# Attention heads divided before their output projection, two heads projected together, and value projections in rounded passes

## The reference

```
xn  = layernorm(x)
out = x + attention(xn) + ffn(xn)
```

## Time and profile before

| | |
|---|---|
| median of 3 runs (lowest, highest) | 1462.79 us (1461.44, 1465.05) |
| profiled execution, own time | 1463.13 us |
| its span, first to last instruction | 1461.4 us |
| mean clock granted to TensorE | 0.958 |
| PE, DVE, ACT, POOL busy, share of the span | 92%, 71%, 65%, 59% |
| DMA: bytes moved, mean rate | 72.47 MB, 50 GB/s |

### The profile page before, as it was taken

One profiled execution on the slowest core, in us unless ns is written; L12 is line 12 of the kernel. 1 busy time (PEld: TensorE's weight loads), 2 busy tenths in 40 slices (PEclk: granted clock), 3 DMA queues, 4 the chain that ended last, 5 costly groups with the idle time before them and its releaser, 6 DMA issues.

```text
span 1461.4 us, 27770 instructions
## 1 busy us (share of the span) xinstructions
PE 1351.4 (92%) x8360; PEld 1124.9 (77%) x8361; DVE 1038.1 (71%) x2674; ACT 947.8 (65%) x2094; POOL 867.2 (59%) x1304
## 2 busy tenths in 40 slices
PE   4569998999879999999999899899899999899998
PEld 4446666999757888788788788788788788788886
DVE  5656654222257788888888888888888888888773
ACT  2435544555447677677777677677677777677775
POOL 3426651332227568667667667767766766766666
PEclk9669999999869999999999999999999999999999
DMA  6222221222122022112112212112212212211112
GB/s 204 89 60 63 63 54 55 77 75 77 47 57 52 3 41 50 29 30 51 35 33 44 43 30 46 38 36 42 41 30 46 42 32 39 48 30 32 30 30 59
DMA packets 131078, 72.47 MB, mean 50 GB/s; under 512 B 80216, under 2 KB 116864, under 8 KB 130944
## 3 DMA queue, kind: packets, MB, share of 16 engines
q1 hardware_dynamic: 114304, 54.18, 18.2%
q0 software_dynamic: 4096, 8.40, 1.9%
q10 hardware_dynamic: 12544, 8.29, 1.9%
HBM read 20.47 MB, written 16.52 MB: 25 GB/s over the span
## 4 chain that ended last, share of the span: by engine, by line
PE 53%; DVE 11%; issue 5%; ACT 2%; DMA 1%; SPq 0%; DVEq 0%; POOLq 0%; ACTq 0%
PE max_ps L1281 8%; PE score_ps L1299 6%; PE score_ps L1298 6%; PE misc_ps L1341 6%; PE head_ps L1318 5%; PE head_ps L1327 5%; PE head_ps L1325 5%; PE head_ps L1323 5%; DVE max_ps L1140 4%; PE misc_ps L1262 3%; DVE x_row L1156 2%; PE misc_ps L1256 2%; DVE q_a L1126 1%; PE misc_ps L1257 1%; PE misc_ps L1258 1%
## 5 line engine op out<-in xcount | busy, mean ns | idle before, releaser
L1032 POOL TENSOR_TENSOR p_lo<-probs,p_hi 128x512 fp32r<-128x512 f32 (+3 forms) x560 | 536.1, 958 | 188.5 <-ACT p_hi L1084 183.9
L1082 ACT ACTIVATE probs<-score_ps 128x512 f32<-128x512 f32 (+3 forms) x768 | 377.5, 492 | 257.0 <-PE score_ps L1299 243.8
L1140 DVE CUSTOM_DVE_ANT_0 max_ps<-max_ps,mask 128x128 f32<-128x128 f32 (+7 forms) x512 | 390.7, 763 | 111.1 <-PE max_ps L1281 87.8
L1298 PE MATMUL score_ps<-q_a,k_a 128*128 128x512 f32 (+3 forms) x768 | 304.3, 396 | 0.2 <-ACT p_hi L1084 0.2
L1281 PE MATMUL max_ps<-k_a,q_a 128*128 128x512 f32 (+3 forms) x768 | 238.6, 366 | 54.2 <-DVE shift L1140 45.0
L1024 POOL TENSOR_SCALAR_AFFINE_SELECT probs<-probs 128x128 f32<-128x128 f32 x512 | 153.7, 300 | 202.3 <-ACT p_hi L1084 136.9
L1299 PE MATMUL score_ps<-q_b,k_b 65*128 65x512 f32 (+3 forms) x768 | 269.6, 351 | 0.0
L1084 ACT ACTIVATE p_hi<-score_ps 128x512 fp32r<-128x512 f32 (+3 forms) x560 | 263.1, 470 | 0.0
L1318 PE MATMUL head_ps<-probs,v_all 128*65 128x128 f32 (+3 forms) x1088 | 248.7, 310 | 0.0
L1281 PEld LDWEIGHTS max_ps<-k_a,q_a 128*128 128x128 f32 x768 | 140.8, 195 | 114.9 <-DVE shift L1140 86.5
L1323 PE MATMUL head_ps<-p_hi,v_hi 128*65 128x512 f32 (+3 forms) x560 | 210.3, 376 | 0.0
(11 more groups left out here) (165 smaller groups left out, 2086.6 us busy)
## 6 DMA issues: line engine op xcount, KB each, us to landing
k_a<-k_a SPq DMA_DIRECT2D x64, 256.0 KB
q_b<-q_a SPq DMA_DIRECT2D x64, 256.0 KB
q_b<-shift SPq DMA_DIRECT2D x512, 0.5 KB
sorted_x<-zeros SPq DMA_DIRECT2D x13, 384.0 KB, 5.0
rows<-sorted_x SPq DMA_DIRECT2D x39, 128.0 KB, 2.1
sorted_y<-result ACTq DMA_DIRECT2D x39, 128.0 KB, 1.8
acc<-in_L_attn_x_dram SPq DMA_DIRECT2D x4, 512.0 KB, 7.2
x_row<-in_L_attn_x_dram SPq DMA_DIRECT2D x8, 256.0 KB
```

What stands on the lines that cost most here:

```text
L1032: pool.tensor_tensor(p_lo[:, lo_slot(g, c), w0:w1], probs[:, slot, w0:w1], p_hi[:, slot, w0:w1].bitcast(F32), ALU.subtract).then_inc(pool_ ...
L1082: ins = act.activation(probs[:, slot, 0:width], src[:, 0:width], ACT.Exp, scale=SCALE)
L1140: dve.tensor_tensor_reduce(out=max_ps[:, at:at + width], in0=max_ps[:, at:at + width], in1=mask[:, SEQ - width:SEQ], scale=-1.0, scalar=-M ...
L1298: pe.matmul(dst, k_a[i][s][:, keys], q_a[i][s][:, qs], start=True, stop=False)
```

## The change

- A window's result leaves `head_ps` as `raw`, and its sums are divided out before the projection. SP moves the row of 1024 sums onto 128 partitions (`sums`, step 5 of the next window), VectorE inverts them there (`invert`, step 8), SP moves them back into the row (`inverse`, step 10), and at step 0 of the window after SP copies this row to 64 partitions (`spread`: 64 x 4 KiB, all from one source partition). At steps 3 and 4 GpSimd multiplies `raw` by it, half the columns each time, into the lower or upper 64 partitions of `stacked` (`norm`).
- Both heads of a batch, then on 128 partitions, are projected together in the odd windows at steps 7 and 9 (`project_pair`, 8 fp32 matmuls of 128 rows for both heads), and VectorE adds each 128 x 512 result to `acc` in one operation. The last two windows of either attention call keep the old way (`wo_last`, `last_y`).
- The value projection multiplies rounded parts: three matmuls for each one before (`nT_hi` x `wqkv_hi`, `nT_hi` x `wqkv_lo`, `nT_lo` x `wqkv_hi`); the split of the weights covers the value columns too, so a pair's raw weights are loaded and split earlier.
- Projections of queries and keys go by halves of the tokens, with the copies of a half behind them (8 copies of 128 KiB, in two groups, for 4 of 256 KiB). At the start of a call only four maxima stand ahead of the first score, the other four beside its first two steps.
- The last batch is stored in three parts.

```diff
+            raw = sb(ph2, "raw", [HEAD + 1, 2, SEQ])
+            sums = sb(ph2, "sums", [P, 2, TILES])
+            inverse = sb(ph2, "inverse", [P, 2, TILES])
+            rden_all = sb(ph2, "rden_all", [HEAD, SEQ])
+            stacked = sb(ph2, "stacked", [P, SEQ])
+            wqkv_hi = sb(ph2, "wqkv_hi", [P, 3, P], F32R)
+            wqkv_lo = sb(ph2, "wqkv_lo", [P, 3, P], F32R)
+
+            wo = sb(ph2, "wo", [P, D])
+            wo_last = sb(ph2, "wo_last", [HEAD + 1, 2, D + 1])
...
+            Y_AT = {7: 0, 9: 1}
+            LAST_Y_AT = {8: 0, 10: 1, 11: 2}
...
+            def stacks(W):
+                return W0 <= W < WL - 2
+
+            def beside(W, c):
+                order = []
+                if W < WL:
+                    order.append(("score", W, c))
+                    order += [("max", *item) for item in max_items(W, c)]
+                    if c in PROJECT_AT[W % 2] and W // 2 + 1 < QL:
+                        order.append(("project", W // 2 + 1, PROJECT_AT[W % 2][c]))
+                        order.append(("project_lo", *order[-1][1:]))
+                    if W % 2 and c in Y_AT and stacks(W - 2):
+                        order += [(kind, W // 2 - 1, Y_AT[c]) for kind in ("y", "add")]
+                    if W == WL - 1 and c in LAST_Y_AT:
+                        order += [(kind, W - 1, LAST_Y_AT[c]) for kind in ("last_y", "last_add")]
+                    if c:
+                        order += [("shift", *item) for item in max_items(W, c - 1)]
+                    if stacks(W - 1):
+                        order += [(kind, W - 1, 0) for kind, at in (("sums", 5), ("invert", 8), ("inverse", 10))
+                                  if at == c]
+                    if stacks(W - 2):
+                        order += [(kind, W - 2, n) for kind, n, at in (("spread", 0, 0), ("norm", 0, 3),
+                                                                      ("norm", 1, 4)) if at == c]
+                    unit = W - W0
+                    if native and (unit, c) in SCATTER_AT:
+                        order.append(("scatter", SCATTER_AT.index((unit, c)), 0))
+                    for k, start in enumerate([] if native else STARTS):
+                        if (unit - start, c) in GATHER_AT:
+                            order.append(("gather", GATHER_AT.index((unit - start, c)), k))
+                        order += [("combine", n, k) for n, at_ in enumerate(COMBINE_AT) if at_ == (unit - start, c)]
+                    if W % G == 2 and c == 2 and W // G + 1 < PAIRS:
+                        order.append(("next_weights", W // G + 1, 0))
+                    if W % G == G - 3 and c == 10 and W // G < hps[-1]:
+                        order.append(("weights", W // G + 1, 0))
+                    if W % G == 1 and c == 11 and W - W0 >= G:
+                        order.append(("out_weights", W // G, 0))
...
+            order = ([(kind, Q0, n) for n in range(6) for kind in ("project", "project_lo")]
+                     + [("max", W0, t) for t in range(HALF_TILES)] + [("shift", W0, t) for t in range(HALF_TILES)])
...
+                    def copies(Q, half):
+                        cols = slice(half * BANK, (half + 1) * BANK)
+                        sp.wait_ge(hi_done, Q * 8 + 4 + half * 4)
                         for s in range(2):
-                            k_hi, q_hi = k_a[i][s][0:HEAD, :].bitcast(F32), q_a[i][s][0:HEAD, :].bitcast(F32)
-                            sp.dma_start(k_a[i][s][HEAD:P, :].bitcast(F32), k_hi).then_inc(copies_done, 16)
-                            sp.dma_start(q_b[i][s][0:HEAD, :].bitcast(F32), q_hi).then_inc(copies_done, 16)
+                            k_hi, q_hi = k_a[Q % 2][s][0:HEAD, cols].bitcast(F32), q_a[Q % 2][s][0:HEAD, cols].bitcast(F32)
+                            sp.dma_start(k_a[Q % 2][s][HEAD:P, cols].bitcast(F32), k_hi).then_inc(copies_done[half], 16)
+                            sp.dma_start(q_b[Q % 2][s][0:HEAD, cols].bitcast(F32), q_hi).then_inc(copies_done[half], 16)
...
+                        if kind == "sums":
+
+                            W = g
+                            sp.wait_ge(heads_out[0], W + 2)
+                            sp.wait_ge(heads_out[1], W + 2)
+                            sp.dma_start(sums[:, W % 2], raw[HEAD:HEAD + 1, W % 2]).then_inc(sums_moved[W % 2], 16)
+                        if kind == "inverse":
+                            W = g
+                            sp.wait_ge(sums_inverted, n_stacked(W) + 1)
+                            sp.dma_start(raw[HEAD:HEAD + 1, W % 2], inverse[:, W % 2]).then_inc(inverse_moved[W % 2], 16)
+                        if kind == "spread":
+                            W = g
+                            sp.wait_ge(inverse_moved[W % 2], n_spread(W) * 16)
+                            if W > W0:
+                                sp.wait_ge(norm_done, 2 * n_stacked(W - 1) + 2)
+                            sp.dma_start(rden_all[:],
+                                         raw[HEAD:HEAD + 1, W % 2].unsqueeze(1).broadcast_to([1, HEAD, SEQ])).then_inc(spread[W % 2], 16)
...
+                        for n, (t0, tiles) in enumerate(y_units):
+                            sp.wait_ge(y_added, added[("last_y", WL - 1, n)])
+                            at = (BATCH - 1) * TILES + t0
+                            sp.dma_start(out_tiles[:, at:at + tiles], acc[:, at:at + tiles]).then_inc(stored, 16)
...
+                    def normalise(W, half):
+
+                        s, cols = W % 2, slice(half * BANK, (half + 1) * BANK)
+                        rows = slice(s * HEAD, (s + 1) * HEAD)
+                        if half == 0:
+                            pool.wait_ge(spread[s], n_spread(W) * 16)
+                            if s == 0 and W // 2 > Q0:
+                                pool.wait_ge(misc_ready, place[("y", W // 2 - 1, 1)] + 1)
+
+                        if not native:
+                            pool.wait_ge(pool_split, done[0])
+                        pool.wait_ge(diag_masked, done[1])
+                        pool.tensor_tensor(stacked[rows, cols], raw[0:HEAD, s, cols], rden_all[:, cols],
+                                          ALU.mult).then_inc(norm_done, 1)
+                        pool.wait_ge(norm_done, 2 * n_stacked(W) + half + 1)
...
-                        act.activation(wqk_hi[:], w_raw[:, 0:2], ACT.Copy).then_inc(wqk_hi_done, 1)
+                        act.activation(wqkv_hi[:], w_raw[:], ACT.Copy).then_inc(wqk_hi_done, 1)
...
+                            if half == 0 and W - W0 >= 2:
+                                act.wait_ge(norm_done, 2 * n_stacked(W - 2) + 2)
...
+                    def invert(W):
+                        dve.wait_ge(sums_moved[W % 2], n_spread(W) * 16)
+                        if W - W0 >= 2:
+                            dve.wait_ge(inverse_moved[W % 2], n_spread(W - 2) * 16)
+                        dve.reciprocal(inverse[:, W % 2], sums[:, W % 2]).then_inc(sums_inverted, 1)
+
+                    def after_combine(n):
+                        if n:
+                            dve.wait_ge(comb_step, n)
+
+                    def add_y(Q, n):
+                        u = place[("y", Q, n)]
+                        rows = acc[:, Q % BATCH * TILES + n * GROUP:Q % BATCH * TILES + (n + 1) * GROUP]
+                        dve.wait_ge(misc_ready, u + 1)
+                        dve.tensor_tensor(rows, misc_ps[u % 2][:].rearrange("p (t d) -> p t d", d=D), rows,
+                                          ALU.add).then_inc(y_added, 1)
...
-                                ins = pe.matmul(dst[:, q * P:(q + 1) * P], nT[:, t0:t0 + P], w_raw[:, 2],
-                                                start=True, stop=True)
+                                part = dst[:, q * P:(q + 1) * P]
+                                pe.matmul(part, nT_hi[:, t0:t0 + P], wqkv_hi[:, 2], start=True, stop=False)
+                                pe.matmul(part, nT_hi[:, t0:t0 + P], wqkv_lo[:, 2], start=False, stop=False)
+                                ins = pe.matmul(part, nT_lo[:, t0:t0 + P], wqkv_hi[:, 2], start=False, stop=True)
...
+                    def project_pair(Q, n):
+                        dst = misc_bank("y", Q, n)
+                        pe.wait_ge(norm_done, 2 * n_stacked(2 * Q + 1) + n + 1)
+                        if n == 0:
+                            pe.wait_ge(wout_loaded, Q // BATCH * 16 + 16)
+                        for q in range(GROUP):
+                            q0 = (n * GROUP + q) * P
+                            ins = pe.matmul(dst[:, q * D:(q + 1) * D], stacked[:, q0:q0 + P], wo[:],
+                                            start=True, stop=True)
+                        ins.then_inc(misc_ready, 1)
...
```

580 lines of the change are left out of this document (265 added, 315 removed).

## The result

The changed kernel takes 1788.1 us (median of 4 runs, 1784.3 to 1791.7) against 1462.1 for the kernel before: a ratio of 1.223 (95% interval 1.219 to 1.227). The side was forecast right, the size not: I had said 1600 us, with 1690 as the upper end.

What follows compares the result with a forecast made beforehand. TensorE was taken as the limit, busy 996.2 of 1032.5 us in the late stretch. The sum 1463.1 - 53.8 + 26.9 + 124 + 57 + 11 - 40 + 16 - 6.5 = 1597.7 gave 1600 us, range 1445 to 1690.

Steps and rivals of the forecast that it cites:

- The 10 us: Spread's transfer from one partition to 64: about 10 us, middle of the ratio between 1.3 and 85 us.
- Waits near 2 us bring the clock down now and then; I book 11 us: TensorE's clock loss after new waits: 2 us in a fifth of the pairs, +11 us in all.
- 124 + 57 - 40: Second-call waits: +124 us for late p_lo and masks, +57 through ScalarE, -40 hidden in VectorE's existing combine waits.
- 1.0 us a pair: Two 0.5 us TensorE waits a pair: a late maximum in the even window, and `invert` waiting for `sums`; hidden, not added.
- signs: GpSimd idle several us before products; TensorE's largest waits for p_lo, the mask and step 8's exponentials.
- the second rival: Spread fast, but VectorE waits long on `sums`: 1511 us at 4.5 us landing; chance 0.08 shared with full weight loads.
- GpSimd has 23 of 34.86 us busy in the undisturbed pair, so they fit: Division on GpSimd: 120 products of 1.29 us, 5.2 us a pair, fit its free time; only their start was in question.
- credit of 40 us for combine stalls: New waits at step 8 coincide with VectorE's existing ones: 5 us hidden in each of 8 combine rounds, -40 us.
- the starts, -2.5 us a call: Start of each attention call: copies after one half and half the first maxima beside scores, -2.5 us in each of two.
- My fast case: Spread fast, products never late: 1430 us, 1457 with 1.0 us a pair, named 1440; chances 0.12 faster, 0.07 within 0.3%.
- +26.9: Value projection in twelve rounded matmuls 0.11 us apart: 1.32 us a unit, +0.42, over 64 units +26.9 us.
- 53.8: Output projection of two stacked heads: 16 fewer matmul records in 30 batches at 0.112 us, -53.8 us of TensorE.

Runs made afterwards that it cites:

- best version of the whole change: Kernel with three mends, second call's value projection in fp32 from normed input kept in DRAM and loaded by SP: 1443.8 us, ratio 0.9877 to the kernel before.
- three mends: Changed kernel with inverted sums' row in DRAM, gathers issued in a round's first two windows, eight maxima first at a call's start: 1461.7 us, ratio 0.9988 to before.
- the other combine order: Changed kernel with row in DRAM, eight maxima first, gathers over three windows and 41 later combine steps over five windows instead of three: 1486.9 us.

## Why the prediction was right or wrong

**The mechanism: right in its source, in part in its path.** One partition as the source makes the spread slow (11.2 us from issue to end; I had counted 1.1 + 10), the products come late, and p_lo, ScalarE's copy and the sums behind it. Giving it another source takes 249 us off. The 10 us themselves were partly luck: they are the middle between 1.3 and 85, which no row of the trace could narrow. The rule of the Trainium skill (page "SBUF — State Buffer", section "Door 1: The DMA port swizzle") gave an estimated 9.5 us; the packets give 9.1, so the trace agrees with it, though the sum built on it, 1570, would have been further off.

**The step that failed, first: "Waits near 2 us bring the clock down now and then; I book 11 us".** One undisturbed pair of windows, the same in both kernels, takes 46.47 us with the slow spread and 36.00 with its row in DRAM, with 219 matmul records in each. TensorE's idle time in it is 5.95 against 1.37 us, 4.6 more; its busy time is 40.52 against 34.63, 5.9 more, at a clock of 0.85 against 1.00. I had 0.4 us of clock for such a pair (11 over 27). Over the second call, with the same 6024 records, it takes 1344.49 and 1125.42 us, 219 apart: TensorE's idle time differs by 138 us (231.9 less 93.7), its busy time by 81 (1112.58 less 1031.72). So the clock was 81 us where I had 11. I saw in the earlier trace rows that a single wait of 2.15 us cost another 2, and still booked it for every fifth pair only, though I forecast waits in every window.

**The waits: near as a sum, not term by term.** I had 124 + 57 - 40, less 27 for the 1.0 us a pair, 114 us against the 138. In the undisturbed pair I had 4.6 + 2.1 = 6.7 us of idle time and 5.95 came, but of other parts. TensorE waited 2.2 us for p_lo (I had 3.5 in the two windows), 0.4 for the exponentials (I had 2.1 through ScalarE), and 3.3 for the product itself ahead of the projection at step 7 of the odd window, which is not in my sum: by my own times the product ends near 14 us there, and TensorE came to step 7 at 11.1. TensorE's largest wait over the span was none of those that I named as signs but that for the maxima, which was to be the sign of the second rival. In the second call, the changed kernel, then the one with its row in DRAM:

```profile
PE max_ps L1313 <- DVE shift L1154: 90.1, 45, 9.2
```

```profile
PE max_ps L1316 <- DVE shift L1157: 69.5, 66, 3.0
```

Most of it is there with a fast spread too, and the undisturbed pair has none of it: it belongs to the gathers and the combine windows, which come next.

**Second: "GpSimd has 23 of 34.86 us busy in the undisturbed pair, so they fit".** In a combine pair it was busy 31.02 of 39.73 us, and five more make 36. The gathers stand in that queue, and VectorE waits for the last of them: 67 us, with its clock. It was the order in the queue more than the sum of work, since with the gathers ahead the same products left these pairs at their old length.

**The credit of 40 us for combine stalls hidden behind the new waits: right in kind.** The slow spread costs 181 us in the 24 pairs beside the combine rounds (1148.02 against 966.82 with the row in DRAM), 7.5 a pair, and 10.0 a pair in the two undisturbed ones. With early gathers in both kernels it is 7.5 against 9.6. So 50 to 60 us were hidden, more than I had, but the late gathers took more than that back.

**Third: the starts, -2.5 us a call.** The four maxima beside the first steps cost 5.5 us a call. I priced the copies and the maxima, and did not walk SP's queue at the new start, where shift rows now stand behind copies.

**The sum again with these.** My fast case with its 1.0 us a pair was 1457; 67 for the gathers and 16 for the starts (11 instead of -5) make 1540, and 1539.6 was measured. That it meets so well is luck in part: the price of the values varies between kernels by more than 10 us, as below. The slow spread adds 219 in the second call, and 23 lie ahead of its first score (439.61 less 416.88), where I had 16; that is 242 between the two profiled executions, and 249 between the medians.

**The value projection: right.** 0.11 us apart as read from the scores' loads, 1.29 us a unit instead of 1.32. +26.9 was forecast; alone in the kernel before it is +22, and 17 to 34 in the others, according to who is the limit beside it.

**The output projection: right per record, not as a gain.** Eight records take 0.89 us (four took 0.44 before), and half are gone. But with fp32 values only 0.73 of the 1.76 us arrive in one undisturbed pair (34.13 against 34.86) and 0.1 in the other (34.80). At least 1.0 us a pair is missing, which is what I had booked for the late maximum and for `sums`; that both are its cause was not tested by itself. VectorE still waits 40.0 us for `sums` in that kernel. The best version of the whole change is 18.6 us faster than before, where this part alone was to give 53.8.

**VectorE's relief: right to book nothing.** Its busy time fell by 111 us in the second call (846.06 to 734.71), and TensorE waited longer for it.

## What to carry to other kernels

A row to be laid on many partitions should be read from DRAM or from many partitions; read from one it moved at 29 GB/s here, and VectorE's waits for the 4 KB of sums behind it were 147 us, against 35 with the row in DRAM. Whether new work "fits" on an engine is read from the fullest stretch it falls into, for queued gathers above all. A wait of TensorE that keeps coming back is paid again in its clock, so a forecast of such waits needs a clock term as large as a trace shows for one of them: removing the gathers' gave 24 us of idle time and 46 of busy time. And a late value is followed to every engine that reads it: the projection read the product directly, and no term stood for that.

## What the runs showed of the hardware

- One SBUF partition as a source: 4 KB packets took 2.28 us (1 KB: 0.49), from 64 partitions 0.32, from DRAM 0.16. The time goes with the bytes.
- VectorE's operations between SBUF tiles can be stretched while GpSimd computes: the same 128x128 multiplication took from 0.24 to 3.46 us in one trace. In four traces (before, three mends, the other combine order, products on VectorE) 149 multiplications by gamma, additions of beta and additions to `acc` ran with neither p_lo nor a product of GpSimd beside them, and none took more than 0.37 us. Beside them some took no longer, others up to 3.46. Two groups by form, in the kernel before and then in the one with three mends, where GpSimd has 137 us more to do in the second call:

```profile
L1182 DVE TENSOR_TENSOR x_row<-x_row,fbeta 128x128 f32<-128x128 f32 x32 | 12.9, 403 | 0.3
L1184 DVE TENSOR_TENSOR acc<-acc,x_row 128x128 f32<-128x128 f32 x32 | 9.4, 292 | 1.1
```

```profile
L1196 DVE TENSOR_TENSOR x_row<-x_row,fbeta 128x128 f32<-128x128 f32 x32 | 26.2, 818 | 0.3
L1198 DVE TENSOR_TENSOR acc<-acc,x_row 128x128 f32<-128x128 f32 x32 | 23.4, 732 | 3.5
```
